# A Mamba-style block with a feed-forward gate: another order of its beginning, and two rooms for its last factors

## The reference

```python
xn = layernorm(x)
# scan branch: proj = xn @ in_proj_w.T -> gate, hbc, dt
xBC = silu(causal_conv4(hbc))            # 64 heads of 64, 8 groups, state 128
dt_p = softplus(dt + dt_bias); dA = exp(dt_p * -exp(A_log))
state = state * dA + (dt_p * x)[..., None] * B;  y = state . C + x * D
s = (rmsnorm_per_group(y) * norm_weight * silu(gate)) @ out_proj_w.T
# feed-forward branch, with 8 LoRA adapters of rank 16
g = silu(xn @ W.T + bias + lora(xn))
out = x + s * g
```

## Time and profile before

| | |
|---|---|
| runs | 1854.15, 1856.23, 1857.11 us (median 1856.23) |
| profiled execution, its own time | 1854.72 us |
| its span in the trace | 1852.9 us |
| TensorE busy | 1795.4 us (97%) |
| VectorE, GpSimd, ScalarE busy | 1524.6 (82%), 1156.4 (62%), 831.2 us (45%) |
| mean granted TensorE clock | 0.990 of full speed |

### The profile page before, as it was taken

The page is one execution under the profiler, slowest core; times in us unless marked ns, Lnnn a source line. Parts: engine busy times, 40 slices in busy tenths (PEclk is TensorE's granted clock), DMA queues, the critical chain, the costliest instruction groups (busy, mean ns, idle before and its releaser), DMA issues.

```text
span 1852.9 us, 29427 instructions
## 1 busy us (share of the span) xinstructions
PE 1795.4 (97%) x10904; PEld 1427.2 (77%) x10904; DVE 1524.6 (82%) x1960; ACT 831.2 (45%) x1806; POOL 1156.4 (62%) x1137
## 2 busy tenths in 40 slices
PE   6888999999999999999999999999999999999995
PEld 4766787878778878878777787877878877787874
DVE  6757888888888888888888978888888888888885
ACT  4865444343534444353534444354444435444431
POOL 4125757475575657567688856747574765757478
PEclk9998999999999999999999999999999999999998
DMA  7432423333342333323465333323233333422233
GB/s 243 153 105 74 142 78 134 104 104 104 102 137 102 104 103 103 125 94 134 145 200 190 120 114 106 122 92 118 88 124 109 121 103 103 137 82 101 103 114 125
DMA packets 113502, 220.70 MB, mean 119 GB/s; under 512 B 10448, under 2 KB 46672, under 8 KB 113360
## 3 DMA queue, kind: packets, MB, share of 16 engines
q1 hardware_dynamic: 112320, 218.66, 35.4%
q10 hardware_dynamic: 1040, 0.16, 0.0%
HBM read 204.63 MB, written 14.16 MB: 118 GB/s over the span
## 4 chain that ended last, share of the span: by engine, by line
PE 85%; DVE 5%; POOL 4%; ACT 3%; issue 2%; DMA 1%; SPq 0%; POOLq 0%; DVEq 0%; ACTq 0%
PE ps_conv L1074 9%; PE ps_conv L1077 9%; PE ps_conv L1080 6%; PE ps_y L1219 6%; PE ps_gate L1074 6%; PE ps_gate L1077 6%; PE ps_out L1074 6%; PE ps_out L1077 6%; PE ps_y L1224 5%; PE ps_s L1253 5%; PE ps_gate L1080 4%; PE ps_out L1080 4%; PE turned_x L1174 3%; PE ps_conv L1081 2%; PE ps_g L1231 2%
## 5 line engine op out<-in xcount | busy, mean ns | idle before, releaser
L753 DVE SCALAR_TENSOR_TENSOR xc<-ps_conv,convw_sb,xc 128x511 f32<-128x511 f32 (+2 forms) x576 | 429.8, 746 | 25.4 <-ACT xc L552 11.3
L1009 POOL TENSOR_TENSOR rstd_col<-mean_square,half 128x1 f32<-128x1 f32 x128 | 106.7, 833 | 548.5 <-ACT mean_square L666 548.5
L906 DVE TENSOR_TENSOR decay<-decay,ps_g 128x1024 f32<-128x1024 f32 x128 | 155.9, 1218 | 183.3 <-PE ps_g L1263 183.3
L852 DVE TENSOR_TENSOR_SCAN decay<-decay,eye 128x1024 f32<-128x1024 f32 x128 | 296.5, 2317 | 0.4 <-DMA decay<-decays_d 0.4
L558 ACT ACTIVATE xc<-xc 128x512 f32<-128x512 f32 x192 | 121.3, 632 | 382.5 <-DVE xc L753 381.7
L1027 POOL TENSOR_TENSOR cpre<-cpre,xc 128x1024 f32<-128x1024 f32 x112 | 267.5, 2388 | 0.0
L1074 PE MATMUL ps_conv<-xn_hi,wconv_hi 128*128 128x512 f32 x768 | 243.2, 439 | 0.0
L1077 PE MATMUL ps_conv<-xn_hi,wconv_lo 128*128 128x512 f32 x768 | 207.1, 392 | 0.0
L1219 PE MATMUL ps_y<-decay,dtx 128*64 128x128 f32 x2048 | 197.4, 279 | 2.1 <-DVE decay L906 1.9
L675 ACT ACTIVATE square<-ps_y 128x512 f32<-128x512 f32 x128 | 76.7, 599 | 241.6 <-DVE ps_y L866 241.6
L1074 PEld LDWEIGHTS ps_conv<-xn_hi,wconv_hi 128*128 128x128 f32 x768 | 140.9, 193 | 50.0 <-issue 30.4
(11 more groups left out here) (192 smaller groups left out, 3734.8 us busy)
## 6 DMA issues: line engine op xcount, KB each, us to landing
decay<-decays_d SPq DMA_DIRECT2D x128, 512.0 KB, 5.2
cpre<-rows_d SPq DMA_DIRECT2D x112, 512.0 KB, 3.9
stage<-w_in_t SPq DMA_DIRECT2D x32, 1024.0 KB, 6.6
stage<-w_out_t SPq DMA_DIRECT2D x16, 1024.0 KB, 5.2
stage<-w_in_t SPq DMA_DIRECT2D x32, 256.0 KB, 3.4
out_sum<-hidden SPq DMA_DIRECT2D x16, 256.0 KB, 5.3
ffn_d<-sgate SPq DMA_DIRECT2D x16, 256.0 KB, 2.0
io<-ffn_d SPq DMA_DIRECT2D x16, 256.0 KB, 3.6
```

The costliest lines, as they stand in the source:

```text
L753: e.scalar_tensor_tensor(acc[:, d:], ps[:, 0:BLK - d], convw_sb[:, tile, TAPS - 1 - d:TAPS - d], acc[:, d:], ALU.mult, ALU.add).then_inc(S ...
L852: e.tensor_tensor_scan(d[:, :], d[:, :], eye8[:, :, :].rearrange("p h i -> p (h i)"), 0.0, ALU.mult, ALU.add).then_inc(S["scan"], 1)
L906: e.tensor_tensor(by_head(d[:, :]), by_head(d[:, :]), ps_g[:, P:2 * P].unsqueeze(1).to_broadcast([P, GH, P]), ALU.mult).then_inc(S["M"], 1)
```

## The change

- **Rooms.** The feed-forward weights go into `wout_hi`/`wout_lo`, the step sizes' weights into `ynt_hi`/`ynt_lo` (`dt_hi`, `dt_lo`). So the gate weights can be split in steps 16 to 20, before the feed-forward is through.
- **Order.** There are 26 steps (`STEPS`). The feed-forward product of tile t is in step t+4 instead of t+3. All parts of all four `rate(q)` are in the steps. The four first gate products are there too (20 to 23), alternately in two banks (`gate_bank`). In a step, convolution stands before the feed-forward product.
- **Feed-forward's end.** ScalarE only copies the product out of PSUM into `skip` or `xw` (`ffn_copy`). GpSimd adds the bias into one of four slots. The linear value goes to DRAM; Silu is applied to the fetched tile in the main loop, on ScalarE, at the end of iteration i for f = `finished(i)`.
- **Silu of the convolution** (0 to 5) comes after the last Exp of the step sizes, in steps 20 to 22.
- **DMA order.** Four input tiles, the LoRA factors and the step sizes' weights are fetched before the feed-forward weights, the bias after them.
- **In `rate`**, the last Exp writes to `es` directly, without a copy, and the scan's start values are taken before they are cleared.
- **Last factors.** For f >= 8, odd f use a room of their own in `stage[1]`, so a fetch waits for the tile two before (`fin2 >= f - 1`), and it stands ahead of the store of f-1. Tiles 14 and 15 are finished by VectorE (`fin`). For the last, the product with the factor and the sum with `x` are made before the last output product is complete; two operations follow it. The last sum of squares is made inside the last output product (`yn_lo_ready`).

The diff, cut to what bears on the time:

```diff
-LAG = 4
 DRAIN = 2
-STEPS = TOK + LAG
+CONV_AT, GATE_AT = 14, 20
+STEPS = GATE_AT + CPB + 2
...
-    return range(0, CPB) if i == 0 else range(i + CPB - 1, min(i + CPB, N))
+    return range(i + CPB - 1, min(i + CPB, N)) if i > 0 else ()
...
+def apart(f):
+
+    return f >= NCH and f % 2 == 1
...
+        ffn_room = [skip, xw]
+        dt_hi, dt_lo = ynt_hi, ynt_lo
...
+        def gate_bank(k):
+
+            return ps_y if k < CPB and k % 2 == 0 else ps_gate
...
+        def last_rooms(f):
+
+            if apart(f):
+                return stage[1][:, 0:DM], stage[1][:, DM:2 * DM], S["landed_io_apart"]
+            return io[:, :], x_again[:, :], S["landed_io"]
...
-            return [(q, s - at) for q, at in ((0, 6), (1, 10), (2, 14), (3, 18)) if 0 <= s - at < 7 and s < STEPS]
+            return [(q, s - at) for q, at in ((0, 4), (1, 9), (2, 13), (3, 17)) if 0 <= s - at < 7]
...
-            if RATES[q][0] == 1:
-                return n if n < 3 else n - 1 if n > 3 else None
-            return n if n < 6 else None
+
+            rest = (3, 3, 6, 5)[q]
+            return n if n < rest else n - 1 if rest < n < 7 else None
...
-                    w.wait_ge(S["fin2"], f)
-                w.wait_ge(ffn_st[0], 16 * NCH)
...
+                    w.wait_ge(S["fin2"], f - 1 if f > NCH else f)
...
+                factor, addend, landed = last_rooms(f)
+                e.dma_start(factor, ffn_d[b, c]).then_inc(landed, 16)
+                e.dma_start(addend, hidden[b, c * P:(c + 1) * P, :]).then_inc(landed, 16)
...
-            for dst, src in ((lora_a_sb, lora_a), (lora_b_sb, lora_b_t), (bias_sb, ffn_bias.partition_broadcast(P))):
+            for dst, src in ((lora_a_sb, lora_a), (lora_b_sb, lora_b_t)):
                 e.dma_start(dst, src).then_inc(S["wffn"], 16)
-            e.dma_start(ffn_raw, w_ffn_t.rearrange("(t p) c -> p t c", p=P)).then_inc(S["landed_ffn"], 16)
+            norm_fetch(2)
+            norm_fetch(3)
             for i in range(2):
                 e.dma_start(dt_raw[:, :, i * HEADS:(i + 1) * HEADS],
                             in_cols(INNER + CONV, HEADS)).then_inc(S["landed_dt"], 16)
-            for t in range(2, NCH):
+            e.dma_start(ffn_raw, w_ffn_t.rearrange("(t p) c -> p t c", p=P)).then_inc(S["landed_ffn"], 16)
+            e.dma_start(bias_sb, ffn_bias.partition_broadcast(P)).then_inc(S["landed_bias"], 16)
...
+                for q, n in rate_part(s - 1):
+                    rate(q, part_of(q, n))
...
+                if s == 20:
+                    fetch_decays(0)
+                if s == 22:
+                    fetch_out(0)
...
+                if f is not None and f > NCH:
+                    fetch_last(f)
                 if i > 0 and finished(i - 1) is not None:
                     store(finished(i - 1))
-                if f is not None:
+                if f is not None and f <= NCH:
                     fetch_last(f)
...
-                if s >= LAG:
-                    t = s - LAG
-                    w.wait_ge(S["biased"], t + 1)
-                    w.wait_ge(ffn_st[t % 2], 16 * (t // 2))
-                    e.activation(ffn_out[t % 2], skip[:, :], ACT.Silu).then_inc(S["ffn_act"], 1)
...
+                if CONV_AT < s <= CONV_AT + MT:
+                    conv(s - 1 - CONV_AT)
+                t = linear_at(s - 1)
+                if t is not None:
+                    w.wait_ge(S["mm_ffn"], KT + t + 1)
+                    w.wait_ge(S["biased"], t - 1)
+                    e.activation(ffn_room[t % 2][:, :], (ps_y if t % 2 == 0 else ps_gate)[:, :],
+                                 ACT.Copy).then_inc(S["ffn_copy"], 1)
+                if s == GATE_AT:
+                    for q, n in rate_part(s):
                         rate(q, part_of(q, n))
...
+                if GATE_AT < s <= GATE_AT + CPB:
+                    gate_silu(s - GATE_AT - 1)
+                if s > GATE_AT:
+                    for q, n in rate_part(s):
+                        rate(q, part_of(q, n))
+                for k in {0: (0, 1, 2), 1: (3,), 2: (4, 5)}.get(s - GATE_AT, ()):
+                    silu(k)
+                if 5 <= s < 5 + KT:
+                    split_conv_x(0, [s - 5])
+                if 9 <= s < 9 + KT:
+                    split_conv_bc(0, [s - 9])
+                if 16 <= s < 16 + XT:
+                    split_gate(0, [s - 16])
+                if s < GATE_AT:
+                    for q, n in rate_part(s):
+                        rate(q, part_of(q, n))
...
+                f = finished(i)
+                if f is not None:
+                    factor, _, landed = last_rooms(f)
+                    w.wait_ge(landed, 32 * landings(f))
+                    e.activation(factor, factor, ACT.Silu).then_inc(S["ffn_act"], 1)
...
-                    e.tensor_tensor(skip[:, :], (ps_y if t % 2 == 0 else ps_gate)[:, :], bias_sb,
-                                    ALU.add).then_inc(S["biased"], 1)
...
+            def fin(f, sums):
+
+                acc = out_sum[:, f % NCH, :]
+                factor, addend, _ = last_rooms(f)
+                w.wait_ge(S["osum"], sums)
+                w.wait_ge(S["ffn_act"], f + 1)
+                e.tensor_tensor(acc, acc, factor, ALU.mult).then_inc(S["fin1"], 1)
+                w.wait_ge(S["fin1"], f + 1)
+                w.wait_ge(S["fin2"], f)
+                e.tensor_tensor(acc, acc, addend, ALU.add).then_inc(S["fin2"], 1)
...
+                    elif u == N - 1:
+                        factor = last_rooms(TOK - 1)[0]
+                        fin(TOK - 1, u - NCH + 1)
+                        w.wait_ge(S["mm_out"], u + 1)
+                        w.wait_ge(S["rstd2"], u + 1)
+                        e.scalar_tensor_tensor(factor, ps_out[:, :], scale, factor, ALU.mult,
+                                               ALU.mult).then_inc(S["last_out"], 1)
+                        w.wait_ge(S["last_out"], 1)
+                        w.wait_ge(S["fin2"], TOK)
+                        e.tensor_tensor(acc, acc, factor, ALU.add).then_inc(S["osum"], 1)
...
+                if u == N - 2:
+                    fin(TOK - 2, u + 1)
...
-                w.wait_ge(S["landed_io"], 32 * (f + 1))
-                e.tensor_tensor(acc, acc, io[:, :], ALU.mult).then_inc(S["fin1"], 1)
+                w.wait_ge(S["ffn_act"], f + 1)
+                e.tensor_tensor(acc, acc, factor, ALU.mult).then_inc(S["fin1"], 1)
...
+                t = linear_at(s - 2)
+                if t is not None:
+                    w.wait_ge(S["ffn_copy"], t + 1)
+                    w.wait_ge(S["landed_bias"], 16)
+                    w.wait_ge(ffn_st[t % CPB], 16 * (t // CPB))
+                    e.tensor_tensor(ffn_out[t % CPB], ffn_room[t % 2][:, :], bias_sb, ALU.add).then_inc(S["biased"], 1)
...
+                if 17 <= s < 17 + XT:
+                    split_gate(0, [s - 17])
...
-                if f is not None:
+                if f is not None and f < TOK - 2:
                     fin_multiply(f)
                     fin_add(f)
...
+                for q, n in rate_part(s):
+                    if part_of(q, n) in (0, 5) and s < GATE_AT:
+                        rate(q, part_of(q, n))
...
+                    b, c = token(t)
...
+                    w.wait_ge(S["ffn_copy"], t - 1)
+                    passes((ps_y if t % 2 == 0 else ps_gate)[:, :], xn_cols(chunk_cols(c)),
+                           weights(wout_hi, wout_lo, slice(0, DM)), KT,
+                           lambda: w.wait_ge(S["lo"], t + 1), lambda: w.wait_ge(S["ffn_lo"], KT), S["mm_ffn"])
+                if GATE_AT <= s < GATE_AT + CPB:
+                    gate(s - GATE_AT)
+                if s == GATE_AT + 2:
+                    turn_xc(0)
+                if s == GATE_AT + CPB - 1:
+                    rate(3, 5)
...
+                if u == N - 1:
+                    sum_squares(u)
+                w.wait_ge(S["lo2"], u + 1)
```

More of the change, by code:

```diff
@@ L114, in finished, with landings @@
     return u // (NCH * GROUPS) * NCH + u % NCH if u >= 0 and group(u) % GROUPS == GROUPS - 1 else None
+def apart(f):
+    return f >= NCH and f % 2 == 1
+def landings(f):
+    return sum(apart(k) == apart(f) for k in range(f + 1))
 def heads_bc(ap, n=HD):
@@ L986, in _ @@
                     norm_rstd(s)
-                if s == 1:
-                    for t in range(KT):
-                        w.wait_ge(S["ffn_wl"], t + 1)
-                        w.wait_ge(S["ffn_wh"], t + 1)
-                        split_lo(wgate_lo, ffn_raw, wgate_hi, [t], S["ffn_lo"])
                 if s == 3:
@@ L1191, in _ @@
-            turn_xc(0)
+            for s in range(STEPS):
+                if 1 <= s <= TOK:
+                    turn_x(s - 1)
+                if s == 2:
+                    w.wait_ge(S["lora_b"], 1)
+                    w.wait_ge(S["wffn"], 32)
+                    for t in range(KT):
+                        w.wait_ge(S["ffn_wl"], t - 1)
```

(15 more changed lines are left out.)

252 lines of the change are left out of this document (105 added, 147 removed).

## The result

The changed kernel took 1833.8 us (median of four runs, from 1832.8 to 1837.0) against 1856.4 us before, a ratio of 0.9883 with a 95% interval of 0.9866 to 0.9900. The gain is 22.6 us; 29 were forecast.

A forecast was written before the change was run, and what follows sets the result against it. TensorE sets the pace from 190 to 911 us; time was missing at both ends. Terms 2 + 5.5 + 18.6 - 3 + 5.7 = 28.8 us off 1854.7 give 1825.9, as median 1827 us; range 1816 to 1843.

The forecast's parts named there:

- the likeliest case: Whole kernel: the forecast itself, 1827 us, range 1816 to 1843 us, chance 0.62.
- the wait for the state under 3 us: Sign, 112 to 190 us: TensorE's wait on L875's successor would be under 3 us.
- the wait near 930 us: Sign in the main loop: one wait of 2 to 4 us, released through ScalarE's tap.
- near 1.00 through 40 to 170 us: Sign: TensorE's granted clock would stay near full speed over this stretch.
- Start: To 29 us: LoRA factors no longer wait for the bias, three tiles turned before the feed-forward weights; 2 us gained.
- Steps: 29 to 111 us: fewer table loads, bias additions off VectorE, less TensorE idle time, clock back; 5.5 us gained.
- The rival with the shared port: Steps: mostly long GpSimd operations make a step 5.2 us against 3.1, losing 32 us, 1859 us; chance 0.05.
- Gates and loop's start: 112 to 190 us: waits for state, gate weights and gate bank shrink, clock mostly returns; 18.6 us gained.
- The 6.3 us: 112 to 190 us: TensorE's wait for the state, put on `rate(3)`, whose VectorE taps waited for ScalarE's tap.
- Middle: Main loop: last factors' Silu wait for landings in ScalarE's order; 3 us lost, bounds 0 and 8.
- The 2.8 us put on f = 2: Main loop: Silu waiting for this tile's landing delays the tap 5.2 us, less slack of 1.2 and 1.2.
- End: Last tiles: last landing, Silu and VectorE operations let the final store go out 5.7 us earlier.

The follow-up runs named there:

- the repetition: The changed kernel run again with no edit; its fourth `mm_u` product came at 166.93 us, against 168.45 us in the first trace.
- the experiment on q = 3: Against the changed kernel, step sizes of the last quarter moved from the steps back into the main loop's first four iterations; 10.2 us slower.
- the last experiment: Changed kernel with bias on VectorE, first gate's Silu earlier, two Silu moved, plus tile s normalized in step s; 3.3 us longer than without the norm edit.

## Why the prediction was right, and by how much it was off

Direction and range held, and the likeliest case was the right one. The sum was 28.8 us and 21.2 came (21.8 in the repetition's trace); start, steps, gates and middle all came out short. Of its signs, ten table loads, the wait for the state under 3 us and the place of the last store came as said. TensorE's idle time in the steps (4.2 us for "under 4") and the wait near 930 us (1.7 for "2 to 4") just missed, and the clock "near 1.00 through 40 to 170 us" did not come: it was 0.98 and 0.97. By its steps:

**Start: 2 forecast, 0.5 found.** The two factors did land earlier, but the LoRA products start 1.3 us later than before. The turn of the second tile now stands ahead of them on TensorE, and its norm stands on VectorE behind the statistics of the third tile. The prediction had no price for that (one line before, then two of the changed kernel):

```profile
9.79 5.82 PE L1149 MATMUL ps_conv<-xc 128*128 128x512 f32 x8 [1.73 <-DVE xc L806]
...
10.19 0.90 PE L1170 MATMUL ps_g<-eye,out_sum 128*128 128x128 f32 x3 [2.24 <-DVE out_sum L780]
11.10 5.70 PE L1245 MATMUL ps_conv<-xc 128*128 128x512 f32 x8
```

The weights to which they are added land at 13.9 us, 1.2 later than before, and the last of these products ends at 16.8 us instead of 15.6. The experiment with the weights first shows that fetching them earlier does not help. How the 0.5 us that are left come about was not taken apart.

**Steps: 5.5 forecast, 3.0 found. This is the term that failed.** The table loads fell as counted. The term was 3.9 us of idle time and 1.6 us of clock. Of the idle time 2.7 us went: 4.2 us are left where 3 were allowed. Of the clock nothing came back: it is 0.98 in this window before and after, and the lower level follows the stall of 3.2 us. For two places of its kind the prediction had an estimate of 1.5 us in all, from VectorE's list alone, and GpSimd's 16 new additions were checked only for GpSimd's own time. Beside them VectorE's operations on SBUF took 1.67 to 1.77 us. The rival with the shared port looked for GpSimd as the loser; here the loser was VectorE. The rival was wrong for the kernel as a whole, but its mechanism is behind the missing part: without the additions the first gate's product comes 2.5 us earlier, with them on VectorE 3.4. The Trainium skill's page "SBUF — State Buffer" (SBUF: two separate sides) names both directions: whichever of the two starts first keeps the shared port pair for the whole instruction, and a VectorE operation with two SBUF inputs competes for it with a GpSimd operation that reads SBUF. The trace agrees: L824 and L827 end 0.54 to 0.56 us behind GpSimd's instruction, and L791, with one input in PSUM, takes 0.68 us throughout.

**Gates and loop's start: 18.6 forecast, 16.8 found (19.0 in the repetition).** The idle time that stays is 2.1 + 1.3 + 2.1 us against 2.4 + 1.2 + 0.9 (the prediction's text has 1 us for the scan, its sum 1.2). The 6.3 us had the cause that the prediction gave, as the experiment on q = 3 shows. The gate's wait is 1.2 us more than forecast, of which 1.0 is L829 beside an addition. The clock is as forecast in the changed kernel's trace, one stretch at the lower level (0.97); the repetition has none (1.00) and 0.7 us less waiting for the second state. So the two traces lie on both sides of the forecast, and 0.8 us of the 1.8 that are missing in the first have no place.

**Middle: -3 forecast, -3.4 found, and -1.2 near the end.** The 2.8 us put on f = 2 came out at 1.9, through the tap, as named; before `mm_u` 54 ScalarE and VectorE waited:

```profile
931.33 0.63 ACT L760 ACTIVATE io<-io 128x512 f32<-128x512 f32 x1 [2.88 <-DMA x_again<-hidden]
...
932.73 2.32 DVE L801 SCALAR_TENSOR_TENSOR xc<-ps_conv,convw_sb,xc 128x511 f32<-128x511 f32 x3 [2.33 <-ACT xc L589]
935.56 3.02 DVE L910 TENSOR_TENSOR_SCAN decay<-decay,eye 128x1024 f32<-128x1024 f32 x1
938.61 1.08 DVE L915 TENSOR_TENSOR last<-decay,prefix_dt 128x8 f32<-128x8 f32 x1
...
941.76 1.10 PE L1336 MATMUL ps_s<-xw,b_tok 128*128 128x512 f32 x2 [1.73 <-DVE state L931]
```

That 1.9 lies so near is partly luck, since two errors offset each other. The fetch did not come 1.5 us later behind GpSimd, so the tap was late by 3.5 us and not by 5.2, which less the slack of 1.2 + 1.2 us leaves 1.1. The scan and `last` took 3.02 and 1.08 us beside GpSimd where they had taken 2.28 and 0.83 at the same place before, 1 us more that the prediction did not have.

The other 1.4 us were not forecast ("the other six tiles have their landing in time"). They had, but GpSimd now waited for the Silu. Its multiplication moved into VectorE's scan (ScalarE's Silu, GpSimd's two operations, VectorE's scan, of the changed kernel):

```profile
973.97 0.62 ACT L760 ACTIVATE io<-io 128x512 f32<-128x512 f32 x1
...
974.73 1.28 POOL L1035 TENSOR_TENSOR out_sum<-out_sum,io 128x512 f32<-128x512 f32 x1 [2.30 <-ACT io L760]
976.10 3.16 POOL L1041 TENSOR_TENSOR out_sum<-out_sum,x_again 128x512 f32<-128x512 f32 x1
...
975.04 3.12 DVE L910 TENSOR_TENSOR_SCAN decay<-decay,eye 128x1024 f32<-128x1024 f32 x1
978.20 1.07 DVE L915 TENSOR_TENSOR last<-decay,prefix_dt 128x8 f32<-128x8 f32 x1
```

In the kernel before, the multiplication had ended when the same scan began, and the scan took 2.28 us:

```profile
992.01 1.31 POOL L969 TENSOR_TENSOR out_sum<-out_sum,io 128x512 f32<-128x512 f32 x1
...
993.40 2.28 DVE L852 TENSOR_TENSOR_SCAN decay<-decay,eye 128x1024 f32<-128x1024 f32 x1
```

That is 0.84 us; another 0.52 is the Silu of the next tile itself, which at 985.4 us stands between four scaled copies and the tap of a convolution for which VectorE then waits 1.55 us instead of 0.20. The same happened at 1777 us: the multiplication, behind its Silu, starts 0.3 us ahead of the scan where it had started 2.7 us ahead, scan 3.11 for 2.28 us and `last` 1.08 for 0.17, and TensorE waited 1.07 us longer. That the collision alone makes these 0.84 and 1.2 us is read from the two traces; no experiment moved it by itself, though with the Silu in the steps all three losses were gone.

**End: 5.7 forecast, 5.8 found**, after 0.4 us lost ahead of it; its working held (the store goes out 1.6 us behind the last product). The last landing, which the prediction took as the bound, had 0.6 us to spare against the last product.

## What to carry to other kernels

Work that moves from one engine to GpSimd, or moves in time there, has to be laid over VectorE's list as well: each pair that comes to overlap can lengthen a VectorE operation on SBUF by about 1 us, even where both engines have time to spare. A wait of TensorE costs more than its length where the granted clock falls behind it, so a forecast that counts on the clock coming back has to show that the longest wait goes. An operation that waits for a transfer is best put where its engine would wait anyway (behind the tap, ahead of the Silu), and whoever waits for it must have room too. And a single trace of the beginning is good to about 1.5 us here, one of the last iterations to 1.9 us; follow one product through both traces, and the place of each gain and loss stands out.

## What the runs showed of the hardware

A VectorE operation on 128x512 elements in SBUF with two inputs there took 0.69 us with GpSimd idle and up to 1.77 us when it started during an operation of GpSimd; one on 128x8 elements took 0.17 us, and 1.07 where it started early in GpSimd's; the scan 2.28 and up to 3.12. One with a single input in SBUF and two scalars (L780, in the last experiment L779) took 0.54 and up to 1.51 us. GpSimd's split took 1.75 for 1.29 us beside the first of them, and its addition 3.16 us beside the scan. Operations of VectorE with an input in PSUM showed nothing of it (L791 0.68, L801 0.75 us throughout). The granted clock fell to the lower level behind TensorE's wait of 3.24 us at 45 us (0.51 from 45.7 to 49.1 us), and did not where the longest wait there was 1.7 us. Table loads leave no gap: at 103.87 us a load of 1.28 us starts, at 105.16 the Ln, at 105.87 the next load, at 107.16 the Exp.
